# Slot stage in four lanes of one group each, with norms, routing and scatter by groups, and the kept slots added on TensorE

## The reference, cut to what matters

```python
slots = q_mu + jnp.exp(q_logsig) * layernorm(x2)
x_in = _ln(ctx, lnkv_g, lnkv_b); k = x_in @ wk + bk; v = x_in @ wv + bv
for _ in range(3):
    prev = slots
    q = _ln(slots, lnq_g, lnq_b) @ wq + bq
    attn = softmax(einsum('bnd,bkd->bnk', k, q) / scale, axis=-1) + 1e-8   # over the 128 slots
    attn = attn / jnp.sum(attn, axis=1, keepdims=True)
    slots = einsum('bnk,bnd->bkd', attn, v) @ wu + bu + prev
    slots = gelu(_ln(slots, lnm_g, lnm_b) @ w1 + b1) @ w2 + b2 + slots
    slots = _ln(slots + cond[:, None, :], lnp_g, lnp_b)
x3 = x2 + slots
z = layernorm(x3); probs = softmax(z @ w_gate + b_gate)
out = x3 + max(probs) * expert_MLP[argmax(probs)](z)                      # "b"
```

## Time and profile before

| | us |
|---|---|
| median of 3 runs (lowest, highest) | 981.83 (980.21, 982.06) |
| profiled execution | 977.38 |
| its span | 975.6 |
| busy PE / DVE / ACT / POOL | 770.0 / 584.4 / 509.1 / 388.4 |

### The profile page before, as it was taken

One profiled execution on the slowest core, in us unless ns is written; L12 is line 12 of the kernel. 1 busy time (PEld: TensorE's weight loads), 2 busy tenths in 40 slices (PEclk: granted clock), 3 DMA queues, 4 the chain that ended last, 5 costly groups with the idle time before them and its releaser, 6 DMA issues.

```text
span 975.6 us, 18523 instructions
## 1 busy us (share of the span) xinstructions
PE 770.0 (79%) x5945; PEld 650.1 (67%) x5945; DVE 584.4 (60%) x1939; ACT 509.1 (52%) x1078; POOL 388.4 (40%) x563
## 2 busy tenths in 40 slices
PE   5898899999999999999777699999363645550692
PEld 5677778788888788887665459998242534340692
DVE  2477778777767666568754443333869687763012
ACT  2566677666677666676444223335364545530461
POOL 1234354333333333332337333656624344225453
PEclk9799999999999999999897799999677677765796
DMA  9592011000011001010001136885300000002463
GB/s 264 182 352 94 1 36 36 14 23 28 2 35 36 15 16 34 2 35 28 14 6 37 68 99 174 253 244 167 106 1 1 0 0 0 0 1 76 127 198 106
DMA packets 43155, 70.95 MB, mean 73 GB/s; under 512 B 5339, under 2 KB 28587, under 8 KB 42651
## 3 DMA queue, kind: packets, MB, share of 16 engines
q1 hardware_dynamic: 39579, 62.64, 21.1%
q0 software_dynamic: 3488, 7.20, 2.1%
HBM read 56.53 MB, written 22.67 MB: 81 GB/s over the span
## 4 chain that ended last, share of the span: by engine, by line
PE 46%; DVE 21%; issue 14%; POOL 9%; ACT 5%; DMA 2%; SPq 2%; DVEq 0%; POOLq 0%; ACTq 0%
PE bank L568 5%; PE bank L839 5%; PE bank L630 5%; PE bank L593 3%; DVE sb_smax L1376 3%; PE bank L583 3%; DVE sb_row_sum L1386 3%; PE bank L618 3%; PE bank L574 2%; PE bank L602 2%; PE bank L847 2%; PE bank L659 2%; PE bank L970 2%; DVE sb_st_all L1680 2%; POOL sb_rstd_all L2052 2%
## 5 line engine op out<-in xcount | busy, mean ns | idle before, releaser
L1954 POOL TENSOR_TENSOR sb_expd<-sb_expd,sb_rden 128x512 f32<-128x512 f32 (+1 forms) x128 | 112.6, 880 | 270.3 <-DVE sb_rden L1390 270.1
L1376 DVE TENSOR_REDUCE sb_smax<-bank 128x4 f32<-128x512 f32 (+1 forms) x128 | 74.1, 579 | 63.6 <-PE bank L593 38.8
L618 PE MATMUL bank<-sb_eye,sb_expd 128*128 128x128 f32 (+1 forms) x512 | 78.2, 280 | 6.9 <-POOL sb_expd L1954 6.2
L1080 ACT ACTIVATE sb_expd<-sb_shifted 128x512 f32<-128x512 f32 (+1 forms) x128 | 69.8, 545 | 21.0 <-DVE sb_shifted L1379 19.6
L1386 DVE TENSOR_REDUCE sb_row_sum<-sb_expd 128x4 f32<-128x512 f32 (+1 forms) x128 | 72.9, 570 | 10.9 <-ACT sb_expd L1080 10.9
L1074 ACT ACTIVATE sb_probT<-bank 128x512 f32<-128x512 f32 (+1 forms) x128 | 74.3, 590 | 9.1 <-PE bank L618 8.8
L618 PEld LDWEIGHTS bank<-sb_eye,sb_expd 128*128 128x128 f32 (+1 forms) x512 | 59.9, 146 | 28.3 <-POOL sb_expd L1954 13.9
L1379 DVE TENSOR_TENSOR sb_shifted<-bank,sb_smax 128x512 f32<-128x512 f32 (+1 forms) x128 | 74.9, 585 | 4.4
L893 PE MATMUL bank<-sb_eye,sb_z_all 128*128 128x128 f32 x96 | 24.3, 420 | 66.9 <-ACT sb_z_all L1168 66.9
L568 PE MATMUL bank<-sb_h1T,sb_watt 128*128 128x128 f32 x512 | 72.6, 289 | 4.5 <-DMA sb_watt<-att_w 2.3
L630 PE MATMUL bank<-sb_probT,sb_v 128*64 128x128 f32 (+1 forms) x1024 | 71.2, 282 | 5.5 <-issue 4.0
(11 more groups left out here) (251 smaller groups left out, 1886.9 us busy)
## 6 DMA issues: line engine op xcount, KB each, us to landing
sb_up_w<-gate_up SPq DMA_DIRECT2D x38, 384.0 KB
rows_a<-pad_a SPq DMA_DIRECT2D x1, 7670.0 KB, 26.8
sb_up_w<-w1b SPq DMA_DIRECT2D x23, 256.0 KB
sb_v<-v_all SPq DMA_DIRECT2D x16, 308.0 KB
v_all<-sb_v_rows SPq DMA_DIRECT2D x9, 512.0 KB, 2.6
sb_blk_x<-rows_a SPq DMA_DIRECT2D x38, 65.0 KB
sb_watt<-att_w SPq DMA_DIRECT2D x4, 512.0 KB, 6.3
sb_picked<-back_a SPq DMA_DIRECT2D x4, 512.0 KB, 5.4
```

Of the source, the lines that this page charges most:

```text
L618: mm = pe.transpose(trans[u % 2][0:n, h, :], expd[:, (units_before(i) + u) % EXP_RING, h, 0:n], eye[:, :])
L1080: act.activation(expd[:, (units_before(i) + u) % EXP_RING, :, 0:n], shifted[:, u % 2, :, 0:n], ACT.Exp, scale=DH ** -0.5).then_inc(exp_don ...
L1376: dve.tensor_reduce(smax[:, u % 2, :], s_in, X, ALU.max).then_inc(max_done, 1)
L1954: pool.tensor_tensor(e, e, rden[:, u % 2, :].unsqueeze(2).broadcast_to([P, QH, n]), ALU.mult).then_inc(norm_done, 1)
```

## The change

The slot stage gets four lanes of one group each, and nothing is a hardware loop any more. All four lists are made from one table, `SLOT_STEPS`: a step of group g in iteration it has the place 4 (it + 1) + g + phase, and each engine takes its own steps in the order of their places. So the lists repeat every unit of 1, in which each engine does each of its steps once, for different groups. Each operation keeps its tiles, but is issued, linked and signalled per group; a root is of 4 columns and not of 8.

- The sum at L1783 goes: in `layer2` PE multiplies the kept slots by the identity into the same PSUM bank, and `measure_o` and `centre` read that bank.
- `normed_here` goes: ACT applies all norms.
- POOL's additions of `picked` to `x` go to VectorE (`add`).
- Gate, choice, rank and place of "b" run per group (`gated`, `choose`, `place`), with the rows of an expert in a region of its own, as for "a"; POOL sends the four tiles of a group when that group is placed (`send`). All of them stand in VectorE's list behind the last `shift_q`. The block table is made behind the last group, and now has the start of each block beside its expert; SP shifts the start to get the expert.
- `rows_b` and `back_b` get room for 8 regions of 16 blocks and 7 blocks more, 135 blocks instead of 23, and the padding table that SP copies into `rows_b` grows with them. The weights `w1b` get a ninth expert of zeros for blocks that hold nothing.
- In `routing` the columns of the one-hot tables are taken at the part's own place, also for "a".

```diff
-NREG = EA * REGION + NR - 2 * TOK // P
-
-PARTS = {"a": ((0, 12), (12, B)), "b": ((0, B),)}
+NREG = {"a": EA * REGION + NR - 2 * TOK // P, "b": EB * REGION + NB - TOK // P}
+
+PARTS = {"a": ((0, 12), (12, B)), "b": tuple((t, t + 4) for t in range(0, B, 4))}
...
+SLOT_STEPS = {
+    (-1,): {"add": 0.84},
+    range(0, SLOT_ITERS + 1): {"measure_q": -1.33, "root_q": -0.46, "shift_q": -1.09, "norm_q": -0.66,
+        "turn_q": -0.51, "scale_q": -0.36},
+    range(SLOT_ITERS): {"logits": 0.14, "max": -0.12, "exp": 0.11, "shares": 0.48, "update": 1.43, "updated": 0.89,
+        "keep_mid": 1.64, "measure_m": 1.02, "root_m": 1.62, "shift_m": 1.32, "norm_m": 1.44, "turn_m": 1.74,
+        "scale_m": 1.69, "layer1": 2.38, "gelu": 1.97, "layer2": 2.45},
+    range(-1, SLOT_ITERS): {"measure_o": 2.22, "root_o": 3.07, "centre": 2.35, "slots": 2.59},
+    range(-1, SLOT_ITERS - 1): {"keep_slots": 5.37},
+    (SLOT_ITERS,): {"gate": 0.29, "gated": 3.30, "choose": 4.09, "rank": 2.28, "choice_exp": 7.01, "place": 4.89,
+        "send": 6.94},
+}
+
+
+def slot_steps(*names):
+    found = [(4 * (it + 1) + g + phases[name], name, it, g) for its, phases in SLOT_STEPS.items() for name in names
+             if name in phases for it in its for g in range(4)]
+    return [step[1:] for step in sorted(found)]
...
+            def place(x, m):
+
+                first = sp.value_load(start[x][0:1, m:m + 1], min_val=0, max_val=NREG[x] - 1)
+                return first, (first >> REGION.bit_length() - 1).with_bounds(min_val=0, max_val=N_EXP[x])
...
+            for step, it, g in slot_steps("turn_q", "logits", "update", "turn_m", "layer1", "layer2", "gate", "rank"):
...
+                if step == "layer2":
+                    pe.wait_ge(mid_rest, nth(it, g))
+                    pe.wait_ge(hid_ready, nth(it, g))
+                    for n, b in enumerate(tiles(g)):
+                        pe.matmul(quads(bank[2 * g])[:, n, :], eye[:, :], s_rest[:, b, :], start=True, stop=False)
+                        mm = pe.matmul(quads(bank[2 * g])[:, n, :], hid[:, b, :], w2s, start=False, stop=True)
                     mm.then_inc(mlp_done, 1)
...
+            for step, it, g in slot_steps("norm_q", "scale_q", "exp", "norm_m", "scale_m", "gelu", "choice_exp"):
...
-                    dve.tensor_tensor(group(S, g), quads(bank[2 * g])[:, :, :], group(s_rest, g), ALU.add).then_inc(sum_ready, 1)
...
-            def normed_here(g, src, dst):
-
-                for b in range(4 * g, 4 * g + 4):
-                    ins = dve.tensor_scalar(dst[:, b, 0:D], src[:, b, :], mv_all[:, b, 0:1], rstd_all[:, b:b + 1],
-                                            ALU.subtract, ALU.mult)
-                ins.then_inc(normed_by_dve, 1)
...
+            def row(src, b):
+
+                return quads(bank[2 * (b // 4)])[:, b % 4, :] if src is SUMS else src[:, b, :]
...
+            of_b = [routing("b", g) for g in range(G)]
+            dve.wait_ge(exp_out["a"], len(PARTS["a"]) + 1)
+            for step, it, g in slot_steps("add", "measure_q", "shift_q", "max", "shares", "updated", "measure_m", "shift_m", 
+                                          "measure_o", "centre", "slots", "gated", "choose", "place"):
+                c = slice(4 * g, 4 * g + 4)
+                if step == "add":
+                    dve.wait_ge(came_back[g], 16)
+                    for k in range(2):
+                        link(dve.tensor_tensor(group(x_sb, g), group(x_sb, g), picked[:, c, k, :], ALU.add))
...
+                if step == "measure_q" and it == SLOT_ITERS:
+                    dve.wait_ge(S_ready, nth(it, g))
+                    dve.tensor_tensor(group(x_sb, g), group(x_sb, g), group(S, g), ALU.add).then_inc(x3_ready, 1)
+                    dve.wait_ge(x3_ready, g + 1)
+                    measured(g, x_sb, "q")
...
+                if step == "measure_o":
+                    if it >= 0:
+                        dve.wait_ge(mlp_done, nth(it, g))
+                    measured(g, x_sb if it < 0 else SUMS, "o")
+                if step == "centre":
+                    scale = es_b[:, :] if it < 0 else R["lnp_g"]
+                    src = x_sb if it < 0 else SUMS
+                    for b in tiles(g):
+                        ins = dve.scalar_tensor_tensor(S[:, b, :], row(src, b), mv_all[:, b, 0:1], scale, ALU.subtract, ALU.mult)
+                    link(ins)
+                if step == "slots":
+                    dve.wait_ge(root_ready["o"], nth(it + 1, g))
+                    stand()
+                    for b in tiles(g):
+                        ins = dve.scalar_tensor_tensor(S[:, b, :], S[:, b, :], rstd_all[:, b:b + 1],
+                                                       R["q_mu"] if it < 0 else R["lnp_b"], ALU.mult, ALU.add)
+                    ins.then_inc(S_ready, 1)
...
+                if step == "gated":
+                    dve.wait_ge(lgb_done, g + 1)
+                    dve.tensor_tensor(logits[:, c, :], bank[2 * g + 1][:, 0:4 * EB].rearrange("p (b e) -> p b e", b=4),
+                                      R["b_gate"].unsqueeze(1).broadcast_to([P, 4, EB]), ALU.add).then_inc(fin_step, 1)
+                    dve.wait_ge(fin_step, g + 1)
+                if step == "choose":
+                    steps(of_b[g], 100)
...
-                for g in LANES[1]:
-                    pool.wait_ge(came_back[g], 16)
-                    pool.tensor_tensor(group(x_sb, g), group(x_sb, g), picked[:, 4 * g:4 * g + 4, k, :],
-                                       ALU.add).then_inc(x2_by_pool, 1)
...
+            def root(k, g, count):
+
+                c = slice(4 * g, 4 * g + 4)
+                pool.wait_ge(var_ready[k], count)
+                pool.tensor_tensor(rstd_all[:, c], rsq_all[:, 0, c], halves[:, c], ALU.pow).then_inc(root_ready[k], 1)
...
+                if step == "keep_slots":
+                    pool.wait_ge(S_ready, nth(it + 1, g))
+                    pool.tensor_tensor(group(s_rest, g), group(S, g), R["bu"].unsqueeze(1).broadcast_to([P, 4, D]),
+                                       ALU.add).then_inc(S_rest, 1)
+                if step == "keep_mid":
+                    pool.wait_ge(mid_ready, nth(it, g))
+                    pool.tensor_tensor(group(s_rest, g), group(S, g), group(cb2, g), ALU.add).then_inc(mid_rest, 1)
+                if step == "send":
+                    pool.wait_ge(routed["b"], g + 1)
+                    pool.wait_ge(z_normed["q"], nth(it, g))
+                    for b in tiles(g):
+                        scatter_one("b", 0, b)
...
+    arr["w1b"] = np.concatenate([I["L1_ffn_W1"], np.zeros((1, D, FB), np.float32)])
```

More of the change, by code:

```diff
@@ L1459, in routing @@
                 yield
[L1460 to L1462 removed]
+                link(dve.tensor_tensor(every(base), every(base), every(R["regions"]), ALU.add))
+                yield
                 if part:
@@ L1753, in updates @@
[L1753 to L1762 removed]
+            links = [0]
@@ L1849, in _ @@
[L1849 to L1859 removed]
+                if step == "measure_m":
+                    dve.wait_ge(mid_ready, nth(it, g))
+                    measured(g, S, "m")
@@ L1861, in expert_of @@
+                if step == "choose":
+                    steps(of_b[g], 100)
+                if step == "place":
+                    steps(of_b[g], 100)
             def expert_of(m):
```

496 lines of the change are left out of this document (148 added, 348 removed).

## The result

The changed kernel takes 984.17 us (median of 7 runs, 983.49 to 985.83) where the kernel before, on the same chip, takes 981.38 (979.91 to 982.06): a ratio of 1.0036, 95% interval 1.0022 to 1.0050. The forecast was 961.1. Its profiled execution took 984.21 us with a span of 982.3.

A forecast was written before the change was run, and what follows sets the result against it. The slot stage was taken as bound by hand-offs, VectorE having most to do, then the seam behind it. First rows 23.1 us earlier plus a 2.4 us stall gave -20.7, from 981.83 to 961.1 us; range 948 to 981.

The forecast's parts named there:

- The stage's length: Slot stage: from VectorE's start at 679.13 to the last shift at 854.7, 15.1 us earlier than before.
- filling: Start of the slot stage: units 2, 3 and 4, not yet full, at 7.3, 8.5 and 10.1 us, to 708.4.
- The unit from VectorE's list: Slot stage: VectorE's steps for one unit sum to 11.5 us and set its length; other engines fit under it.
- PSUM statistics: measure_o in the slot stage: reading statistics from PSUM costs no surcharge, bounds 0 and 0.3 us a unit.
- keep_slots starts just when slots starts.: Slot stage: POOL's addition runs beside VectorE's slots, which then takes 2.1 us a unit, bounds 1.1 and 2.4.
- The loop across the engines: Slot stage: loop over layer2, measure_o, norm, logits, layer1, update: 9.9 us at 2.4 GHz, 13.7 at 1.2; not the bound.
- PE's longest hole: Slot stage: in the new list PE's longest idle stretch is about 2 us.
- Table loads: ACT in the slot stage: two loads a unit, 2.6 us, bringing ACT to 10.3, which fits under 11.5.
- identity products: PE's layer2 in the slot stage: 8 matmuls costing 1.16 to 1.9 us a unit, PE 9.1 to 9.8, which fits.
- The tail: End of the slot stage: the last group alone, latency counting, to 846.9, then 7.8 us to the last shift.
- The seam: From last shift to first rows: four routings 22.3 us, scatters partly overlapped; first rows at 884.7, 23.1 us earlier.
- The padding table: Early phase: 7280 KB more delay the values' load to 106.2; PE stalls 2.4 us, bounds 0 and 6.

The follow-up runs named there:

- e9_mid_only: Changed kernel with GpSimd's keep_mid alone moved ahead of the next group's root_m (phase 1.64 to 1.56); ratio to the kernel before 0.9894.
- e10_slots_only: Changed kernel with GpSimd's keep_slots alone moved behind root_q (phase 5.37 to 4.55); ratio to the kernel before 1.0044.
- e6_update_first: e1_order with TensorE's update moved ahead of layer1 (phase 1.43 to 1.33); 971.71 us, ratio to the kernel before 0.9879.
- e2_no_load: Changed kernel with the slot stage's Gelu replaced by Identity, so no table changes between exp and gelu; 984.1 us, ratio to the kernel before 1.0003.
- e3_no_identity: Changed kernel without the four products with the identity in layer2; 984.7 us, ratio to the kernel before 1.0015.
- e4_late_weights: Changed kernel with the routing weights taken out of place and done for all groups behind the block table; 983.74 us, ratio to the kernel before 1.0003.
- p1_pad: Kernel before with only rows_b, back_b and the padding table lengthened to 135 blocks; 982.04 us, ratio to the kernel before 0.9985.
- e5_one_routing: Changed kernel with one routing for all sixteen tiles behind the last group's gate, all scatters behind it; 985.15 us, ratio to the kernel before 1.0021.
- e11_all: e6_update_first plus late routing weights and early groups' routing steps placed in VectorE's idle stretches; 955.15 us, ratio to the kernel before 0.9743.
- e1_order: Changed kernel with GpSimd's keep_mid moved ahead of root_m and keep_slots behind root_q; 974.77 us, ratio to the kernel before 0.9909.

## Why the prediction was wrong, step by step

- **The stage's length** (forecast 175.6 us, measured 195.9) is the step that failed. Its parts: filling 29.3 forecast, 29.2 measured (682.45 to the first measure_m at 711.64); the nine full units 103.5 against 116.8; the last two 23.5 against 27.1; the last group's tail 19.2 against 22.7. So 17 of the 20 us are the units: 11.5 forecast, 13.0 measured in the mean of the nine full ones (12.2 to 13.6).
- **The unit from VectorE's list.** The list without waits was 12.3 us, 0.8 more than its sum: the three measures take 4.6 us and not 4.2, and the contention is 0.77 on the variance and 0.80 on the shares in place of 1.0 on slots. PSUM statistics cost no surcharge (0.89 against 0.87), as taken.
- **"keep_slots starts just when slots starts."** It starts with the shares, because root_o is done while VectorE is still centring. I had asked which step of VectorE reads two operands from SBUF; the steps that suffered here read one. The Trainium skill (SBUF — State Buffer, Who interferes with whom) says that a VectorE instruction contends with GpSimd when it has two SBUF inputs or runs in a mode that takes both ports, and that tensor_scalar can do so. The rows agree on both sides: variance and shares are tensor_scalar from SBUF to SBUF and are slowed, the statistics with one input are not, nor is the update from PSUM.
- **The loop across the engines** is what the prediction had and set aside, and the one that closes is another. I had a loop that went over layer2 and measure_o, priced it at 9.9 to 13.7 us and took VectorE for the bound. The loop that closes is the one over shift_m, norm_m, turn, logits, layer1 and update, in which VectorE's measures stand too: of VectorE's 13.57 us 3.9 (776.84 to 780.77) and 1.5 (788.87 to 790.41) are in it, and the 8.1 between are ACT's and PE's. The products were in my loop in the right order; what I had wrong is where it goes back to VectorE. From the update it goes through updated, measure_m and measure_o, 5.4 us with the shift, and I had 1.6. My own terms with 5.4 in place of 1.6, and without the two products of layer2, give 11.4 us at the higher level and 13.7 at the lower (an estimate: 5.4 + 1.65 + 0.4 + 0.5 and three products of 1.16 or 1.9). So the loop sets the unit from products of 1.2 us on, not only from 1.5. I had also taken about 2 us for PE's longest hole; it was 3.18 us (782.59), and logits, layer1 and update took 1.9 each behind it. So within the unit this is the step that failed: the loop was put beside VectorE's list and stood above it. e9_mid_only and e10_slots_only show that the loop sets the long units; e6_update_first shortens it.
- **Table loads** and the identity products: at nothing inside the stage, as the sum had them, shown by e2_no_load and e3_no_identity.
- **The tail** of the last group, 3.5 us longer: the wait for layer2 alone is 4.80 us, 16 matmuls from 866.72 to 870.5 at the lower clock, 3.8 us where 2.9 was summed; the rest isn't parted. Nor is the 0.7 us of the last stage followed further.
- **The seam** was to be 30.0 us to the first rows and was 33.3. The four routings took 25.2 us (878.40 to 903.58) and not 22.3, of which 2.04 is the wait for the exp, a cost that I had left out of it; its place is shown by e4_late_weights. The waits for PE's rank products (0.59, 0.59, 0.24, 0.85) are 0.7 more than the four times 0.4 that were summed. Then SP's weights in front of the rows took another 2.1 of landing: I had moved the weights' loads behind the last place, counted their issue and not what they do to the rows' transfer. Against PE's first product the gain is 2.5 us and not 8.
- **The padding table**, 2.4 us of stall forecast, none of it in the time of p1_pad. As a mechanism the step was right: 12 of 13 traces show PE waiting for the values, 0 to 2.5 us more than before. The changed kernel's own trace is the one without it, by its timing: the table's transfer was issued 2.15 us earlier than before (46.56 against 48.71) and landed 54.5 us later where 56.2 were summed; so the values' load left the queue at 102.31, not 106.2, and the product that needs them (107.69) came 1.4 us later than before.

The sum by pieces: stage +5.2 in place of -15.1, seam with landing -2.5 in place of -8.0, last stage +0.7 in place of 0, padding 0 in place of +2.4: +3.4 in place of -20.7.

## What to carry to other kernels

When each engine runs a fixed list, the unit is the longest of the lists and of every loop that goes through several of them. Write the loops down with the order in which each engine does its steps, other groups' steps included; a wait that grows by what a step gives back (here 0.76 to 1.53 us) shows that the step wasn't on the loop. When two engines contend, ask which of the slowed steps is on the loop and move the other engine's step away from that one: one phase changed from 1.64 to 1.56 gave 13.9 us by the ratio and 11.1 by the pieces. And work that is split so that it can overlap gains only if it is put into the holes: four routings one behind the other were worth no more than one, in the holes 6 us more.

## What was not expected of the hardware

- A four-column variance of 0.17 us took 0.94 beside GpSimd's addition of 512 columns, and ended within 0.02 us of it (780.78 and 780.76). A tiny instruction can cost five times its time in this way.
- Beside such an addition, statistics of SBUF took 0.87 us for four tiles as without it, and the update from PSUM (770.16 in e6_update_first, keep_slots from 770.06) 1.13 as without it.
- Rows of 65 KB a block took 4.04 us from the first one's issue to PE behind four weights of 256 KB, and 1.87 to 1.99 alone (e5_one_routing, e11_all).
- Logits, layer1 and update took 4.9 us together in a mean unit of e1_order (clock 0.78 in the window) and 4.2 in one of e6_update_first (0.85), with nothing changed but their order and the waits between them.
- A transfer of 8775 KB that PE's values had to queue behind made PE wait up to 3.04 us for them in an early phase, and p1_pad, which has it and nothing else, isn't slower by more than 0.2 us.
